# Feed-forward tail of a decoder layer: fetches, bias, last scale and expert number moved

## The chip, the cores and the metric

The kernel runs on one NeuronCore of a Trainium2 chip. The metric is device time in microseconds of one execution. The engines are PE (TensorE, matmuls), DVE (VectorE), ACT (ScalarE), POOL (GpSimd) and SP (SyncE, which here only issues DMAs). Each works through its own list of instructions in order; semaphores tie them together.

## The reference

A decoder layer: self-attention, cross-attention, and a feed-forward block with a choice of two of eight experts per token, each followed by a residual sum and a layer norm. There are 16 x 100 = 1600 tokens of width 512. What the change touches is the last part:

```
logits = x @ router_w + router_b                 # [tokens, 8]
topk_vals, topk_idx = top_k(logits, 2)
full_w = softmax weights of the two, 0 elsewhere
h = einsum('td,edf->etf', x, expert_w) + expert_b
combined = einsum('etf,te->tf', silu(h), full_w)
out = combined @ proj_w + proj_b
y = x + out
ffn = norm_w * (y / sqrt(mean(y * y) + 1e-6))
result = layernorm(x + ffn)
```

## The kernel before

`build` runs three phases one behind the other, with all engines meeting in between: `self_attention_phase`, `cross_attention_phase` and `feed_forward_phase`. Only the third concerns us in detail. Its input x2 lies in HBM. It has these stages.

**Routing.** PE transposes x2 and makes the logits; DVE ranks them, counts tokens per expert and gives each (token, choice) a slot. The slots fill NJ = 32 tiles of 128, and all slots of a tile belong to one expert, whose number is in `te_s`. In the meantime the weights are loaded and each is split in a high and a low fp32r half (`Ehl`, `Phl`); a product of two split matrices takes three matmuls (high x high, low x high, high x low).

**Expert stage**, a loop over the 32 tiles. POOL gathers the tile's rows of x2 by an indirect DMA (`gather_slots`, three buffers). PE transposes them (L1304, four at 128x128), ACT casts the result to the high half (`slots_hi`, L1364), DVE makes the low half (`slots_lo`, L1514). PE's iteration j is: transposes of tile j+1, a wait for the low half of tile j (`g_lo`), the load of the expert's number into a register (`value_load`, L1314), then four quarters (`c`) of three matmuls each (L1317 to L1319), whose weights are addressed by that register. DVE adds the expert's bias (L1526), ACT takes Silu (L1373), SP stores the tile to `y_d` in HBM (L1247). ACT's order is: high half of tile j+1, Silu of tile j.

**Output stage**, a loop over NT = 13 tiles of tokens (the last has 64). It begins when all 32 tiles have been stored. SP loads x2 once more (`x2r`, four DMAs, L1251), and with it the bias `pb_s` and the norm weight `nw_s`, each spread over 128 partitions (L1253, L1254). POOL gathers the two expert results of each token (`gather_results`, L1604, two indirect DMAs per tile). The steps on a tile t are, with their engine:

- ACT: `weigh_first` (L1378), weight of the first result; DVE: `combine` (L1532), adds the second one weighted
- PE: `transpose_combined` (L1326); ACT: `combined_hi` (L1384); DVE: `combined_lo` (L1538)
- PE: `product3` (L65), twelve matmuls with 512 columns
- POOL: `biased_residual` (L1610), x2 plus bias; DVE: `residual` (L1545), adds the product
- ACT: `square` (L1390), with a sum over the row; POOL: `rms` (L1615, L1617), adds eps and takes the power -0.5 of a single column
- DVE: `rms_norm` (L1551 to L1558), scale, x2 added, statistics; POOL: `ln` (L1622, L1624), the same for the variance
- DVE: `layer_norm` (L1563), subtracts the mean and scales; SP: store to the output (L1257)

The order on each engine is written out by hand, as a software pipeline. In step t DVE does combine(t+1), combined_lo(t), residual(t-1), rms_norm(t-2), layer_norm(t-3). POOL issues the gathers of tiles 0 to 2, then biased_residual(0) and (1), then in step t gather(t+3), biased_residual(t+2), rms(t-1), ln(t-2). The tiles of the output stage lie where the expert weights were, so they can be filled only after the last expert matmul.

## Time and profile before

| | us |
|---|---|
| median of 3 runs (lowest, highest) | 1701.53 (1699.75, 1701.56) |
| the profiled execution | 1697.03 |
| its span | 1695.2 |
| mean granted clock of PE | 0.94 of full |
| PE busy | 1492.5, 88% of the span |
| DVE busy | 1001.7, 59% |
| POOL busy | 688.0, 41% |
| ACT busy | 647.0, 38% |

The profile is of one execution. All times inside it count from the first instruction. Shares over the whole span say little about a change at the end of the program; the feed-forward phase begins near 1371 us, its expert stage runs from 1475 to 1591, and its output stage from there to the end. Matmuls overlap in the records: with 0.39 each they start 0.23 apart.

### The profile page before, as it was taken

Reading aid. Unit: us, or ns where it says so; the run is one execution under the profiler, and the core shown is the slowest. Engines: PE = TensorE matmul, PEld = TensorE weight load, DVE = VectorE, ACT = ScalarE, POOL = GpSimd, SP = SyncE. Lnnn points to the kernel's source line nnn. Section 1 sums busy time; section 2 is a strip of 40 time slices with the busy share of each in tenths; the row PEclk is TensorE's granted clock in tenths of the full one; section 3 lists DMA queues with packets and bytes.
Section 4 is the critical chain, followed back from the end, with each engine's and each line's share of the span. In section 5 each row is a group of like instructions: output and inputs, shape, how many; then the busy total and the mean of one; then the engine's idle time right before and its main releaser. Section 6 shows DMA issues by size and latency. Waiting matters only on the chain. (4 is left out here: it accounts for less than half of the span.)

```text
span 1695.2 us, 27877 instructions
## 1 busy us (share of the span) xinstructions
PE 1492.5 (88%) x8420; PEld 1227.9 (72%) x8420; DVE 1001.7 (59%) x3594; ACT 647.0 (38%) x1744; POOL 688.0 (41%) x1041
## 2 busy tenths in 40 slices
PE   7999999999975899999999999999999962599665
PEld 6778787787754678788887878878788862477443
DVE  3765666656654755566565666555566517633388
ACT  4433434434321544344444344444344413233222
POOL 1343332423323544444444434444444207422186
PEclk9999999999987999999999999999999965599788
DMA  6212112121115311111111111111111044255532
GB/s 215 98 51 97 68 68 87 58 96 58 73 69 173 115 52 62 57 53 47 57 56 59 59 53 49 55 57 61 57 57 47 31 139 181 74 149 149 196 112 84
DMA packets 59538, 143.21 MB, mean 84 GB/s; under 512 B 7038, under 2 KB 17890, under 8 KB 58459
## 3 DMA queue, kind: packets, MB, share of 16 engines
q1 hardware_dynamic: 54878, 127.36, 22.1%
q0 software_dynamic: 4576, 14.95, 3.5%
q8 instruction: 27, 0.44, 0.1%
q14 instruction: 57, 0.46, 0.1%
HBM read 97.85 MB, written 44.43 MB: 84 GB/s over the span
## 5 line engine op out<-in xcount | busy, mean ns | idle before, releaser
L65 PE MATMUL b_bank<-b_kTh,b_q 128*100 128x362 f32 x512 | 172.0, 337 | 6.6 <-DVE b_nmax L963 4.0
L876 ACT ACTIVATE b_probs<-b_probs,b_nmax 100x361 f32<-100x361 f32 x256 | 151.8, 593 | 65.6 <-DVE b_nmax L963 64.4
L1064 POOL TENSOR_TENSOR b_pcarry<-b_half 128x1 f32<-128x1 f32 x176 | 41.7, 237 | 314.5 <-DVE b_rinv L969 261.3
L963 DVE CUSTOM_DVE_ANT_0 b_probs<-b_bank,b_mask 100x361 f32<-100x361 f32 x256 | 135.5, 529 | 50.7 <-issue 39.6
L1089 POOL TENSOR_SCALAR b_probs<-b_probs,b_rinv 100x361 f32<-100x361 f32 x256 | 158.3, 631 | 0.0
L956 DVE TENSOR_TENSOR b_pTl<-b_bank,b_pTh 121x400 fp32r<-121x400 f32 x192 | 110.0, 573 | 50.2 <-ACT b_pTh L871 48.8
L871 ACT ACTIVATE b_pTh<-b_bank 121x400 fp32r<-121x400 f32 x192 | 96.7, 504 | 100.3 <-PE b_bank L740 99.2
L903 ACT ACTIVATE b_oTh<-b_bank,b_bv 128x400 fp32r<-128x400 f32 x64 | 38.1, 595 | 209.5 <-PE b_bank L65 209.5
L740 PE MATMUL b_bank<-b_ident,b_probs 100*121 100x100 f32 x768 | 110.7, 267 | 4.9 <-POOL b_probs L1089 4.9
L740 PEld LDWEIGHTS b_bank<-b_ident,b_probs 100*121 100x121 f32 x768 | 108.5, 187 | 7.3 <-POOL b_probs L1089 6.3
L65 PE MATMUL b_bank<-b_Woh,b_oTh 128*100 128x512 f32 x256 | 108.1, 422 | 1.4 <-DVE b_oTl L1028 1.4
L65 PEld LDWEIGHTS b_bank<-b_kTh,b_q 128*100 128x100 f32 x512 | 85.2, 166 | 28.0 <-issue 9.5
L1028 DVE SCALAR_TENSOR_TENSOR b_oTl<-b_bank,b_bv,b_oTh 128x400 fp32r<-128x400 f32 x64 | 40.5, 633 | 107.9 <-ACT b_oTh L903 107.9
L65 PE MATMUL a_bank<-a_Wqh,a_x1Th 128*100 128x512 f32 x256 | 101.5, 396 | 2.7 <-DVE a_qn L472 1.5
L65 PE MATMUL a_bank<-a_Wqh,a_x1Tl 128*100 128x512 f32 x256 | 101.6, 397 | 0.0
L65 PE MATMUL a_bank<-a_Wql,a_x1Th 128*100 128x512 f32 x256 | 101.3, 396 | 0.0
L65 PE MATMUL b_bank<-b_Wol,b_oTh 128*100 128x512 f32 x256 | 101.1, 395 | 0.0
L65 PE MATMUL b_bank<-b_Woh,b_oTl 128*100 128x512 f32 x256 | 101.0, 394 | 0.0
L65 PE MATMUL b_bank<-b_Wkh,b_ctxh 128*121 128x512 f32 x192 | 83.8, 437 | 14.6 <-DVE b_Wkl L918 14.6
L357 ACT ACTIVATE a_probs<-a_probs,a_nmax 100x100 f32<-100x100 f32 x256 | 92.8, 365 | 4.4 <-DVE a_nmax L425 4.4
L540 POOL TENSOR_TENSOR a_probs<-a_probs,a_rinv 100x400 f32<-100x400 f32 x64 | 54.7, 855 | 95.0 <-DVE a_rinv L432 95.0
L65 PE MATMUL b_bank<-b_kTl,b_q 128*100 128x362 f32 x256 | 84.4, 330 | 0.0
(238 smaller groups left out, 4066.0 us busy)
## 6 DMA issues: line engine op xcount, KB each, us to landing
q_d<-a_qo SPq DMA_DIRECT2D x64, 400.0 KB, 2.4
b_q<-q_d SPq DMA_DIRECT2D x64, 400.0 KB, 3.1
b_ctxr<-in_ctxT SPq DMA_DIRECT2D x48, 242.0 KB, 4.0
c_stage<-in_expert_w SPq DMA_DIRECT2D x16, 512.0 KB, 5.9
y_d<-c_y SPq DMA_DIRECT2D x32, 256.0 KB
a_stage<-in_Wq SPq DMA_DIRECT2D x4, 1024.0 KB, 5.6
b_stage<-in_Wo SPq DMA_DIRECT2D x8, 512.0 KB, 3.5
...
```

The costliest lines, as they stand in the source:

```text
L65: mm = eng.matmul(out, lhsT=l(c), rhs=r(c), start=first and k == 0, stop=last and k == n - 1)
L357: e = act.activation(probs[:, r, c, :], probs[:, r, c, :], ACT.Exp, scale=-1.0, bias=nmax[:, h:h + 1], accum_out=psums[:, r, c:c + 1])
L540: pool.tensor_tensor(probs[:, r], probs[:, r], rinv[:, r].unsqueeze(2).to_broadcast([S, DC, S]), ALU.mult).then_inc(pn_rdy, 1)
L740: mm = pe.transpose(t_bank[c % 2][0:KT, h * S:(h + 1) * S], probs[:, s % 2, h, c * KT:(c + 1) * KT], ident_s[0:S, 0:S])
L871: act.activation(pTh[:, c, :], t_bank[c % 2][0:KT, 0:XG * S], ACT.Copy).then_inc(pt_hi, 1)
L876: act.activation(p, p, ACT.Exp, scale=-1.0, bias=nmax[:, s % 2, h:h + 1], accum_out=psums[:, s % 2, h:h + 1]).then_inc(e_rdy, 1)
L903: act.activation(oTh[:, kv, :], o_bank[:, 0:XG * S], ACT.Identity, bias=bv_s[:, kv:kv + 1]).then_inc(o_hi, 1)
L956: dve.tensor_tensor(pTl[:, c, :], t_bank[c % 2][0:KT, 0:XG * S], pTh[:, c, :].bitcast(F32), ALU.subtract).then_inc(pt_lo, 1)
L963: dve.tensor_tensor_reduce(out=probs[:, s % 2, h, 0:SE], in0=s_bank[h % 2][0:S, 0:SE], in1=mask_s[:], scale=-1.0, scalar=BIG, op0=ALU.add, ...
L1028: dve.scalar_tensor_tensor(out=oTl[:, kv, :], in0=o_bank[:, 0:XG * S], scalar=bv_s[:, kv:kv + 1], in1=oTh[:, kv, :].bitcast(F32), op0=ALU.add,
L1064: pool.tensor_tensor(pcarry[:, k:k + 1], half_s[:, 0:1], half_s[:, 0:1], ALU.add)
L1089: pool.tensor_scalar(p, p, rinv[:, s % 2, h:h + 1], 1.0, ALU.mult, ALU.mult).then_inc(p_rdy, 1)
```

## The change

Five edits, all but one within `feed_forward_phase`:

- **x2.** The first three tiles (`x2a`) are loaded during the expert stage, behind the first store; the other ten (`x2b`) after it in three DMAs of three tiles and one of the rest. `residual` waits per group of three tiles.
- **Bias.** `pb_s` is one row. ACT casts it and a row of ones after the second Silu (behind a wait for both loads), DVE makes the low half, and each product gets two more matmuls with a contraction of one row (`ones_r` x `pbh`, `ones_r` x `pbl`). `biased_residual` is gone; `residual` adds x2 to the product.
- **Small steps.** The two additions of eps move from POOL to DVE (`mean_square` and the end of `rms_norm`); POOL keeps the two powers, with ln ahead of rms.
- **Last scale.** ACT does it, with a scale and a shift; DVE makes the shift, one column (`mean_shift`).
- **Expert number.** The load for tile j+1 stands ahead of the last quarter of tile j.

The semaphores of the first phase are cleared on POOL ahead of the second and given back ahead of the third. Several tiles now share memory with ones used up earlier.

```diff
+            def expert(j):
+                return pe.value_load(te_s[0:1, j:j + 1], min_val=0, max_val=E - 1)
+
             transpose_slots(0)
+            e_next = expert(0)
             pe.wait_ge(w_lo, NP)
             for j in range(NJ):
+                e = e_next
                 if j + 1 < NJ:
                     transpose_slots(j + 1)
                 pe.wait_ge(g_lo, j + 1)
                 wait(pe, h_rdy, j - 1)
-                e = pe.value_load(te_s[0:1, j:j + 1], min_val=0, max_val=E - 1)
                 for c in range(DC):
+                    if c == DC - 1 and j + 1 < NJ:
+                        e_next = expert(j + 1)
...
@@ SP @@
-                if j == NJ - 1:
-                    sp.wait_ge(h_done, NJ)
-                    for k in range(4):
-                        sp.dma_start(held(x2r, k), four_tiles(x2_f, k)).then_inc(x2r_in, 16)
-                        if k == 0:
-                            sp.dma_start(pb_s[:], proj_b.partition_broadcast(P)).then_inc(tail_in, 16)
-                            sp.dma_start(nw_s[:], norm_w.partition_broadcast(P)).then_inc(tail_in, 16)
+                if j == 0:
+                    sp.dma_start(pb_s[:], proj_b.rearrange("(a d) -> a d", a=1)).then_inc(tail_in, 16)
+                    sp.dma_start(nw_s[:], norm_w.partition_broadcast(P)).then_inc(tail_in, 16)
+                    sp.dma_start(x2a[:], x2_f[0:3 * P, :].rearrange("(t p) d -> p t d", p=P)).then_inc(x2_in[0], 16)
+            sp.wait_ge(h_done, NJ)
+            for k in range(3):
+                sp.dma_start(x2b[:, 3 * k:3 * k + 3], x2_f[(3 + 3 * k) * P:(6 + 3 * k) * P, :].rearrange("(t p) d -> p t d", p=P)).then_inc(x2_in[k + 1], 16)
+            sp.dma_start(x2b[0:rows(NT - 1), NT - 4], x2_f[(NT - 1) * P:B * S, :]).then_inc(x2_in[0], 16)
...
@@ PE, output stage @@
-                         lambda c: Phl[:, 0, c, :], lambda c: Phl[:, 1, c, :], range(DC)).then_inc(p_done, 1)
+                         lambda c: Phl[:, 0, c, :], lambda c: Phl[:, 1, c, :], range(DC), last=False)
+                pe.matmul(p_bank[t % 2][0:n, :], lhsT=ones_r[:, 0:n], rhs=pbh[:], start=False, stop=False)
+                pe.matmul(p_bank[t % 2][0:n, :], lhsT=ones_r[:, 0:n], rhs=pbl[:], start=False, stop=True).then_inc(p_done, 1)
...
@@ ACT @@
+                if j == 1:
+                    act.wait_ge(tail_in, 32)
+                    act.activation(ones_r[:], ones_s[0:1, :], ACT.Copy).then_inc(pb_split, 1)
+                    act.activation(pbh[:], pb_s[:], ACT.Copy).then_inc(pb_split, 1)
...
+            def layer_norm(t):
+                n = rows(t)
+                act.wait_ge(shift_set, t + 1)
+                act.activation(u_s[0:n, t], u_s[0:n, t], ACT.Identity, scale=rstd[t][0:n, :], bias=shift[t][0:n, :]).then_inc(o_rdy, 1)
...
@@ DVE @@
-                dve.wait_ge(x2p_set, t + 1)
-                dve.tensor_tensor(u_s[0:n, t], p_bank[t % 2][0:n, :], u_s[0:n, t], ALU.add).then_inc(u_rdy, 1)
+                if t == NT - 1:
+                    dve.wait_ge(x2_in[0], 48)
+                elif t % 3 == 0:
+                    dve.wait_ge(x2_in[t // 3], 32)
+                dve.tensor_tensor(u_s[0:n, t], p_bank[t % 2][0:n, :], x2_tile(t), ALU.add).then_inc(u_rdy, 1)
...
+            def mean_square(t):
+                n = rows(t)
+                dve.wait_ge(sq_done, t + 1)
+                dve.tensor_scalar(rr[t][0:n, :], ss[t][0:n, :], D * RMS_EPS, None, ALU.add).then_inc(ms_set, 1)
...
+                dve.wait_ge(mv_set, t + 1)
+                dve.tensor_scalar(rstd[t][0:n, :], mv[t][0:n, 1:2], LN_EPS, None, ALU.add).then_inc(var_set, 1)
...
+            def mean_shift(t):
+                n = rows(t)
+                dve.wait_ge(rstd_set, t + 1)
+                dve.scalar_tensor_tensor(out=shift[t][0:n, :], in0=mv[t][0:n, 0:1], scalar=-1.0, in1=rstd[t][0:n, :], op0=ALU.mult,
+                                         op1=ALU.mult).then_inc(shift_set, 1)
...
@@ POOL @@
-            pool.wait_ge(tail_in, 32)
-            biased_residual(0)
-            biased_residual(1)
             for t in range(NT + 2):
                 if t + 3 < NT:
                     gather_results(t + 3)
-                if t + 2 < NT:
-                    biased_residual(t + 2)
+                if 2 <= t:
+                    ln(t - 2)
                 if 1 <= t <= NT:
                     rms(t - 1)
-                if t >= 2:
-                    ln(t - 2)
...
@@ build @@
+        for handle in first:
+            nc.gpsimd.sem_clear(handle)
         cross_attention_phase(nc, sem, a["ctxT"], a["Wk"], a["Wv"], a["Wo"], a["bk"], a["bv"], a["mask"],
                               a["ident"], x1_d, q_d, x2_d)
+        for handle in first:
+            nc.release_semaphore(handle)
```

In the lists below a row is a line of the kernel, an operation, what it writes and reads (`c_te` holds the expert numbers, `c_xg` the gathered slots, `c_xgh` and `c_xgl` their two halves, `c_Ehl` the expert weights) and its size. The lines of the changed kernel have other numbers. On PE, at the border between two expert tiles, there stood before:

```order
L1317 MATMUL c_bank<-c_Ehl,c_xgh 128x512
L1318 MATMUL c_bank<-c_Ehl,c_xgl 128x512
L1319 ISA
L1319 MATMUL c_bank<-c_Ehl,c_xgh 128x512
L1304 MATMUL c_bank<-c_ident,c_xg 128x128 x4
L1314 TENSOR_LOAD c_te
L1314 ISA x2
L1317 ISA
L1317 MATMUL c_bank<-c_Ehl,c_xgh 128x512
```

and stands now:

```order
L1336 MATMUL c_bank<-c_Ehl,c_xgh 128x512
L1319 TENSOR_LOAD c_te
L1319 ISA x2
L1334 ISA
L1334 MATMUL c_bank<-c_Ehl,c_xgh 128x512
L1335 MATMUL c_bank<-c_Ehl,c_xgl 128x512
L1336 ISA
L1336 MATMUL c_bank<-c_Ehl,c_xgh 128x512
L1315 MATMUL c_bank<-c_ident,c_xg 128x128 x4
L1334 ISA
L1334 MATMUL c_bank<-c_Ehl,c_xgh 128x512
```

The load went from behind the transposes to ahead of the last three matmuls of the tile before.

On DVE one step of the output stage was (`c_r` results, `c_bank` the product, `c_u` the row under way, `c_small` single columns, `c_x2r` and `c_x2b` copies of x2):

```order
L1532 SCALAR_TENSOR_TENSOR c_r<-c_r,c_small 128x512
L1538 TENSOR_TENSOR c_cTl<-c_bank,c_cTh 128x512
L1545 TENSOR_TENSOR c_u<-c_bank,c_u 128x512
L1551 SCALAR_TENSOR_TENSOR c_u<-c_u,c_small,c_nw 128x512
L1554 TENSOR_TENSOR c_u<-c_u,c_x2r 128x512
L1556 BN_STATS c_stat<-c_u 128x6
L1558 BN_AGGR c_small<-c_stat 128x2
L1563 TENSOR_SCALAR c_u<-c_u,c_small 128x512
```

and is now:

```order
L1569 TENSOR_TENSOR c_cTl<-c_bank,c_cTh 128x512
L1584 TENSOR_SCALAR c_small<-c_small 128x1
L1579 TENSOR_TENSOR c_u<-c_bank,c_x2b 128x512
L1604 SCALAR_TENSOR_TENSOR c_small<-c_small 128x1
L1590 SCALAR_TENSOR_TENSOR c_u<-c_u,c_small,c_nw 128x512
L1593 TENSOR_TENSOR c_u<-c_u,c_x2b 128x512
L1595 BN_STATS c_stat<-c_u 128x6
L1597 BN_AGGR c_small<-c_stat 128x2
L1599 TENSOR_SCALAR c_small<-c_small 128x1
L1563 SCALAR_TENSOR_TENSOR c_r<-c_r,c_small 128x512
```

The last wide operation is gone (it is on ACT), and three operations of one column have come in.

On POOL the beginning of the output stage was:

```order
L1591 DMA c_xg<-x_d,c_tok 128x512 x32
L1604 DMA c_r<-y_d,c_slot 128x512 x6
L1610 TENSOR_TENSOR c_u<-c_x2r,c_pb 128x512 x2
L1604 DMA c_r<-y_d,c_slot 128x512 x2
L1610 TENSOR_TENSOR c_u<-c_x2r,c_pb 128x512
L1604 DMA c_r<-y_d,c_slot 128x512 x2
L1610 TENSOR_TENSOR c_u<-c_x2r,c_pb 128x512
L1615 TENSOR_TENSOR c_small<-c_small 128x1
L1617 TENSOR_TENSOR c_small<-c_small 128x1
```

and is now:

```order
L1636 DMA c_xg<-x_d,c_tok 128x512 x32
L1649 DMA c_r<-y_d,c_slot 128x512 x10
L1655 TENSOR_TENSOR c_small<-c_small 128x1
L1649 DMA c_r<-y_d,c_slot 128x512 x2
L1660 TENSOR_TENSOR c_small<-c_small 128x1
L1655 TENSOR_TENSOR c_small<-c_small 128x1
L1649 DMA c_r<-y_d,c_slot 128x512 x2
```

The ten gathers of tiles 0 to 4 now follow each other directly, and two operations of one column per tile remain.

## Rows read from the trace of the kernel before

**Rows 1.** Windows: length; PE, PEld, DVE, ACT, POOL busy (count); clock, DMA share, GB/s.

```profile
1482.00:1590.00 108.00, 101.36 (x485) 80.58 (x483) 41.52 (x60) 33.84 (x61) 25.12 (x27) 1.00 0.50 142
...
1621.00:1672.00 51.00, 36.34 (x137) 26.60 (x138) 50.18 (x67) 15.14 (x34) 45.66 (x59) 0.87 0.37 115
```

**Rows 2.** Timeline of PE, expert stage: start us, us, engine line, [idle before <-releaser].

```profile
1488.09 0.47 PE L1317 MATMUL c_bank<-c_Ehl,c_xgh 128*128 x1
...
1491.96 0.49 PE L1317 MATMUL c_bank<-c_Ehl,c_xgh 128*128 x1 [0.43 <-issue]
...
1495.18 0.47 PE L1317 MATMUL c_bank<-c_Ehl,c_xgh 128*128 x1
```

**Rows 3.** PE sequencer at the lines L1314 and L1317: durations ns, first and last start.

```profile
L1314 PEldq TENSOR_LOAD <-c_te x1: 859/859/859, 1490.7 to 1490.7; - x1
...
L1317 PEldq FUSED_REGOPS  x1: 46/46/46, 1488.8 to 1488.8; - x1
```

**Rows 4.** Timeline, same stretch: what feeds the PE's next tile.

```profile
1495.13 0.69 DVE L1526 TENSOR_TENSOR c_h<-c_bank,c_eb 128x512 f32<-128x512 f32 x1 [1.33 <-PE c_bank L1319]
...
1497.01 0.69 DVE L1514 TENSOR_TENSOR c_xgl<-c_bank,c_xgh 128x512 fp32r<-128x512 f32 x1 [1.18 <-ACT c_xgh L1364]
```

**Rows 5.** Timeline of PE: first matmul of expert tiles 1 and 31.

```profile
1481.03 0.48 PE L1317 MATMUL c_bank<-c_Ehl,c_xgh 128*128 x1
...
1586.90 0.49 PE L1317 MATMUL c_bank<-c_Ehl,c_xgh 128*128 x1
```

**Rows 6.** Timeline at expert tiles 0 and 1, then DMA issue by line, us to landing.

```profile
1482.35 3.52 SPq L1247 DMA_DIRECT2D y_d<-c_y  x2
...
1484.89 0.63 ACT L1373 ACTIVATE c_y<-c_h 128x512 f32<-128x512 f32 x1 [2.09 <-DVE c_h L1526]
...
c_nw<-in_norm_w SPq DMA_DIRECT2D x1, 256.0 KB, 6.8
```

**Rows 7.** Timeline at the start of the output stage.

```profile
1610.75 2.53 POOL L1610 TENSOR_TENSOR c_u<-c_x2r,c_pb 128x512 f32<-128x512 f32 x2 [9.15 <-DMA c_x2r<-x_d]
...
1612.13 0.69 DVE L1545 TENSOR_TENSOR c_u<-c_bank,c_u 128x512 f32<-128x512 f32 x1 [2.82 <-POOL c_u L1610]
...
1613.43 0.97 POOL L1604 DMA_INDIRECT c_r<-y_d,c_slot  x1
...
1618.12 0.72 ACT L1378 ACTIVATE c_r<-c_r,c_small 128x512 f32<-128x512 f32 x1 [4.53 <-DMA c_r<-y_d,c_slot]
...
1618.87 2.30 DVE L1532 SCALAR_TENSOR_TENSOR c_r<-c_r,c_small 128x512 f32<-128x512 f32 x1 [6.04 <-ACT c_r L1378]
```

**Rows 8.** Timeline of DVE and POOL, one tile of the output stage.

```profile
1629.91 2.14 DVE L1563 TENSOR_SCALAR c_u<-c_u,c_small 128x512 f32<-128x512 f32 x1
1630.48 1.27 POOL L1610 TENSOR_TENSOR c_u<-c_x2r,c_pb 128x512 f32<-128x512 f32 x1
...
1632.17 0.98 POOL L1617 TENSOR_TENSOR c_small<-c_small 128x1 f32<-128x1 f32 x1
...
1634.12 1.33 POOL L1604 DMA_INDIRECT c_r<-y_d,c_slot  x1 [0.18 <-issue]
...
1636.06 0.18 DVE L1558 BATCH_NORM_AGGREGATE c_small<-c_stat 128x2 f32<-128x6 f32 x1
...
1636.16 2.15 DVE L1563 TENSOR_SCALAR c_u<-c_u,c_small 128x512 f32<-128x512 f32 x1
```

**Rows 9.** Chain that ended last: start us, us, what; then POOL's drain at the end.

```profile
1675.12 0.65 DVE c_r L1532
...
1690.21 0.54 DVE c_u L1563
...
L1132 POOLq DRAIN  x1: 5406/5406/5406, 1689.6 to 1689.6; - x1
```

**Rows 10.** POOL and its queue where the second phase begins.

```profile
530.04 0.19 POOL L1064 TENSOR_TENSOR b_pcarry<-b_half 128x1 f32<-128x1 f32 x1 [12.65 <-DMA b_ctxr<-in_ctxT]
...
L76 POOLq EVENT_SEMAPHORE  x2: 17/17/17, 526.3 to 526.4; - x2
```

72 lines of the change are left out of this document (40 added, 32 removed).

## The prediction, made before the changed kernel was run

> **What bounds the kernel now.** I read the windows by stage first. The last phase starts near 1371 us, and the change touches only its last two stages: the expert stage (32 tiles of slots) and the output stage (13 tiles of tokens). In the expert stage PE is busy 101 of 108 us at the full granted clock; in the output stage DVE is busy 50.2 of 51 us while PE has 36 and POOL 46 [rows 1]. So PE sets the first and DVE the second.
>
> Next I read the PE timeline of two expert tiles. The tile that starts at 1488.09 lasts 3.87 us and the next 3.22, the long one with a gap of 0.43 before the following tile's first matmul that nothing in the profile releases ("issue") [rows 2]. PE's sequencer shows why. The load of the expert's number starts at 1490.7 and takes 0.86 us [rows 3]; with the two register operations behind it the first matmul comes 1.25 us after the load's start. The load stands behind the wait for the low half of the tile's own slots. In the tile that PE starts at 1495.18, DVE takes up the result of the one before at 1495.13 and, after ACT, has the next low half ready at 1497.01 + 0.69 = 1497.70 [rows 4], 2.52 us into a tile that needs 3.22. A load that starts only then shows its first matmul at 1498.95 at the earliest, 0.6 late. A tile delayed in this way gives the following load more time, which then hides. Hence a long and a short tile in turn. First matmuls run from 1481.03 to 1586.90, 30 tiles in 105.87 us, 3.53 each [rows 5].
>
> In the output stage I read the timeline at its start and in its middle. At the start POOL stands at the sum of x2 and bias until all of x2 has landed (9.15 us idle, ends 1610.75), and the gathers for tile 3 are queued behind it: they are issued at 1613.43, ACT gets the data at 1618.12, and DVE, idle for 6.04 us, goes on at 1618.87 [rows 7]. In the middle a DVE step repeats every 6.25 us (1629.91 to 1636.16). Of it 2.14 is the last scale L1563, beside POOL's L1610 of 1.27 [rows 8]; with POOL quiet the same line takes 0.54 [rows 9]. The rest of the step is 4.10.
>
> **The expert number, part by part.** The load now stands ahead of the last quarter of the tile before. At that point the sequencer is ahead of the array: the register operation of the last quarter is at 1488.8 in the short tile [rows 3], and its matmul comes nine matmuls after 1488.09, about 1490.24, so the lead is 1.4 us against a cost of 1.2 (the load and what follows up to the next dispatch). Then the wait for DVE no longer holds up a load, only matmuls, and it ends some 0.7 us before the PE has finished the tile before. Every tile should take the short 3.22: 30 x 3.22 = 96.6, a gain of 9.3, and 0.65 once more for the first tile, together 10.0. Nothing else becomes late: DVE's low half comes 2.52 us into a tile of 3.22 [rows 2, 4].
>
> **Loads and casts in the expert stage.** SP issues three more DMAs behind the first store (1482.35), and ACT, after the second Silu (1484.89, 0.63), waits for two of them and then casts a row of ones and the bias. Norm weights took 6.8 us to land, next to 3 MB of x2 [rows 6]. The issue now falls at about 1483, with little traffic, so I take 4 us (bounds 3 and 6.8). ACT then waits about 1.5 to 2 us, works 0.8, and queued behind it is the high half of tile 3, on which DVE's low half and PE hang. Of about 2.8 us the slack of 0.65 is hidden: cost 2.2 once (bounds 0.2 and 5). SP's stores behind it have two tiles of time. The early x2 load (768 KB) is hidden by PE-bound tiles. The 58 semaphore clears on POOL at the start of the second phase are new. POOL waits there from 526.4 to 530.04 for a DMA anyway; at 17 ns, the nearest row, they take 1.0 us, and at 62 ns they would fill the 3.6 [rows 10]. I take nothing, upper bound 2.
>
> **Start of the output stage.** POOL no longer stops at the bias, so it issues the gathers of tiles 0 to 4 one after another; those of tile 3 have landed by about 1608. The first residual waits for PE rather than POOL, and the two one-row matmuls per tile cost 2 x 0.23 at full clock (a twelfth of a short tile less its transposes; bound 0.43 each at half). I leave it at 1612.2 [rows 7]. Then ACT squares tile 0 (up to 0.8) after DVE's 0.69, weighs tile 3 (0.72), and DVE combines it at about 1614.5 in place of 1618.87: gain 4.3. PE needs 12 x 0.23 + 0.46 = 3.2 us for product 1 from about 1612.5, so it is ready as DVE comes to residual 1, and what is late next is the DVE step itself.
>
> **The DVE step.** It loses 2.15 (L1563 goes to ACT, which is busy 15 of 51 us [rows 1] and has room for 0.7 per 4.7). It gains three one-column operations. The aggregate L1558 starts 0.10 before its successor [rows 8], and a dependent one costs about twice that: 0.5 together (bounds 0.3 and 0.75). That makes 4.10 + 0.5 = 4.6. POOL's step is near that too: two gathers (1.33 and 0.97 with gaps of 0.3), a power beside a DVE operation 0.98, the other about 0.57 [rows 7, 8], 4.45. PE needs 0.35 + 14 x 0.23 = 3.6, at half clock about 7. I take 4.75. In the profile combines 3 and 12 stand at 1618.87 and 1675.12 [rows 7, 9], nine steps of 6.25; at 4.75 the gain is 13.5 (bounds 4.4 and 5.3: 16.6 and 8.5).
>
> **The end.** From combine 12 to the end of the span are 20.1 us, of which the last 5.4 are POOL's drain, after the last power [rows 9]. Four steps each lose 0.54 and gain 0.5, and with no combine left the powers on POOL are not covered: two or three waits of 0.6. Cost 1.5 (bounds 0 and 3).
>
> A rule bears on the step. The rows show one-column powers of POOL stretched (0.98) beside DVE, and DVE's wide operations not. The Trainium skill (SBUF — State Buffer, "SBUF: two separate sides") says that the port pair DVE and GpSimd share is held for a whole instruction, also between a DVE operation with two SBUF inputs and a GpSimd one that reads SBUF, and that the loser blocks whoever it is. By it DVE too would wait for powers that start first, and the sum would be the third rival's below.
>
> **Sum.** -10.0 + 2.2 - 4.3 - 13.5 + 1.5 = -24.1 us. Against the profiled execution of 1697.03 (span 1695.2 and 1.8 around it) that is 1672.9. The median of the runs shown is 4.5 higher, 1701.53, so the forecast is 1677.4.
>
> **The rivals.** First, the load stays exposed: if the matmuls are held not by the load but by the low half itself, long and short tiles remain and 10.0 comes back: 1687.4. For it speaks that the load starts right at DVE's end; against it that the short tile shows 1.25 us between the two. Chance 0.12.
>
> Second, POOL's ring limits the step. The mean square on DVE releases a power, behind it stand two gathers, then 4.7 us from the pair's start to the weighing [rows 7], then the combine, in two steps. That is 1.4 + 0.7 + 4.7 + 0.7, near 8 of 9.5, with 0.5 more by stretches. Should the data land 2.5 later, the step is 5.3: 9 x 0.55 = +5.0, 1682.4. Chance 0.12.
>
> Third, DVE blocks behind POOL's powers, about 0.57 in each of 12 steps: +6.8, 1684.2. Against it: DVE's wide operations beside L1617 are not longer in this profile. Chance 0.08.
>
> Fourth, the block on DVE just moves from L1563 to another line, so the step stays 6.25: +13.5, 1690.9. Against it: the blocker L1610 is gone altogether. Chance 0.04.
>
> Fifth, slower: the load stops PE inside each accumulation. If the sequencer has hardly any lead before the last quarter (0.1 us), 31 tiles lose 1.1 us each, +34: 1711.5. It decides from a lead under 0.4 us, where 31 x 0.8 eats the whole sum. The short tile's lead of 1.4 speaks against it [rows 3]. Chance 0.04. By the Trainium skill (TensorE: Matmul & The Clock Gate, the table at its head) PE's queue holds 64 instructions, which would leave room for such a lead; the row shows a lead of six matmuls and their weight loads.
>
> Last, 0.05 for better than 1670 (step 4.4, no stop of ACT, earlier landings), and 0.55 for the forecast.
>
> **How the numbers follow.** The range runs from 1670 to 1689: the forecast with its bounds and the first three rivals, 0.87 less some for bounds that add up. A measurement of this kernel can tell about 0.2% (3.4 us) from no change. Faster by more than that is every case but the fifth and a sliver: 0.94; within, 0.02; slower, 0.04.
>
> **What would show it.** Expert tiles all near 3.2 us with no "issue" gap, load starts well before DVE's low half; one gap of about 2 us at tile 3. In the output stage no DVE wait of 6 us before combine 3, a step of 4.75, no operation of DVE over 1 us, POOL nearly full. The prediction is wrong if a gap appears before the last quarter of each tile, if ACT waits for r data in each step, or if PE falls to its lower clock through the output stage.

## The result

The changed kernel takes 1681.15 us (median of 4 runs, 1676.13 to 1681.73) against 1700.64 for the kernel before, measured beside it (4 runs, 1698.10 to 1701.56): ratio 0.9881, interval 0.9859 to 0.9904, 19.5 us less. The same pair, measured once more with the experiments, gave 1677.78 (5 runs, 1671.51 to 1683.35) against 1702.01 (11 runs), ratio 0.9846 (0.9826 to 0.9866), 24.2 us less. The forecast was 1677.4, in a range from 1670 to 1689. The first result lies 3.8 above it and the second 0.4; both are in the range.

One execution of each measurement was profiled; the last column of the table is that of the second one. The first of the changed kernel took 1681.01 us (span 1679.2). Where a stage starts and ends was read from the timeline in the same way for both. The marks are the barriers between phases, the start of the first matmul of the expert stage and of the last one on its first line (L1317, now L1334), and the combines on DVE, which count the output tiles.

| stage, us | before | changed | changed, again |
|---|---|---|---|
| first two phases, to the barrier's end | 1371.0 | 1378.1 | 1380.5 |
| last phase to first expert matmul | 104.3 | 102.9 | 103.5 |
| expert stage | 113.8 | 107.3 | 107.0 |
| to combine 0 | 14.4 | 14.4 | 14.4 |
| combine 0 to combine 3 | 15.4 | 10.5 | 10.3 |
| combine 3 to combine 12 | 56.1 | 44.3 | 44.2 |
| combine 12 to the last barrier's end | 20.1 | 21.6 | 21.5 |
| last phase in all | 324.1 | 301.0 | 300.9 |

The last phase lost 23.1 us. Phases one and two, in which only the semaphore clears are new, seem to have taken 7.1 back; below it turns out that most of this is scatter, the profiled execution of before being the fastest one of its kernel.

Windows of the changed kernel by stage, the expert stage and then combine 3 to 12 (length; PE, PEld, DVE, ACT, POOL busy with counts; clock, DMA share, GB/s); they answer to [rows 1]:

```profile
1481.00:1588.30 107.30, 104.56 (x501) 86.20 (x502) 42.87 (x62) 36.88 (x65) 26.50 (x28) 0.96 0.54 155
1613.20:1657.50 44.30, 40.76 (x169) 27.96 (x168) 40.24 (x89) 22.83 (x45) 30.86 (x33) 0.96 0.47 133
```

PE still sets the expert stage (104.6 of 107.3 busy), at a granted clock of 0.96 of full. In the output stage DVE is busy 40.2 of 44.3 us, no longer all of it, and PE's share has gone up to 40.8. PE's idle times end with DVE's combine, so DVE still sets the step, but PE is close behind.

Timeline of PE in the expert stage, the first matmul of tiles 2 to 5 (answers to [rows 2]):

```profile
1489.72 0.48 PE L1334 MATMUL c_bank<-c_Ehl,c_xgh 128*128 x1
...
1495.88 0.49 PE L1334 MATMUL c_bank<-c_Ehl,c_xgh 128*128 x1 [2.73 <-DVE c_xgl L1545]
...
1500.67 0.48 PE L1334 MATMUL c_bank<-c_Ehl,c_xgh 128*128 x1
...
1503.84 0.48 PE L1334 MATMUL c_bank<-c_Ehl,c_xgh 128*128 x1
```

The last two are 3.17 apart, and the tiles from there on come every 3.17 to 3.22: the long ones and the "issue" gaps of [rows 2] are gone. One gap stands out, 2.73 us before the tile at 1495.88, and that tile lasts 4.79 although nothing waits in it: the clock record shows half clock (1.2 GHz) for 3.4 us, from 0.4 behind the gap's end. The load itself, as PE's sequencer had it before (L1314) and has it now (L1319), durations in ns as minimum, median and maximum:

```profile
L1314 PEldq TENSOR_LOAD <-c_te x32: 307/848/863, 1474.4 to 1586.1; - x32
```

```profile
L1319 PEldq TENSOR_LOAD <-c_te x32: 297/302/499, 1478.2 to 1583.5; - x32
```

Timeline of ACT and DVE around the gap (answers to [rows 4] and [rows 6]):

```profile
1490.40 0.63 ACT L1393 ACTIVATE c_y<-c_h 128x512 f32<-128x512 f32 x1 [2.06 <-DVE c_h L1557]
...
1493.71 0.31 ACT L1396 ACTIVATE c_ones_r<-c_ones 1x128 fp32r<-1x128 f32 x1 [2.67 <-DMA c_nw<-in_norm_w]
1493.92 0.61 ACT L1397 ACTIVATE c_pbh<-c_pb 1x512 fp32r<-1x512 f32 x1
1494.44 0.57 ACT L1384 ACTIVATE c_xgh<-c_bank 128x512 fp32r<-128x512 f32 x1
...
1495.05 0.69 DVE L1545 TENSOR_TENSOR c_xgl<-c_bank,c_xgh 128x512 fp32r<-128x512 f32 x1 [4.67 <-ACT c_xgh L1384]
```

ACT waits 2.67 us for the norm weight (issued at 1488.59, so landed 5.1 later), casts, and only then makes the high half, behind which DVE's low half and PE's next tile stand, in the order that the prediction gave.

Timeline at the start of the output stage (answers to [rows 7]):

```profile
1611.13 0.69 DVE L1579 TENSOR_TENSOR c_u<-c_bank,c_x2a 128x512 f32<-128x512 f32 x1 [3.71 <-PE c_bank L1358]
...
1612.49 0.71 ACT L1402 ACTIVATE c_r<-c_r,c_small 128x512 f32<-128x512 f32 x1
...
1613.23 0.75 DVE L1563 SCALAR_TENSOR_TENSOR c_r<-c_r,c_small 128x512 f32<-128x512 f32 x1 [1.41 <-ACT c_r L1402]
```

The wait of 6.04 us before combine 3 is gone, and ACT weighs tile 3 with no wait for data. Timeline of one undisturbed step in the middle, DVE with one POOL power (answers to [rows 8]):

```profile
1648.34 0.74 DVE L1563 SCALAR_TENSOR_TENSOR c_r<-c_r,c_small 128x512 f32<-128x512 f32 x1
...
1648.51 0.99 POOL L1660 TENSOR_TENSOR c_small<-c_small 128x1 f32<-128x1 f32 x1 [0.40 <-DVE c_small L1599]
...
1652.86 0.15 DVE L1599 TENSOR_SCALAR c_small<-c_small 128x1 f32<-128x1 f32 x1
1652.93 0.74 DVE L1563 SCALAR_TENSOR_TENSOR c_r<-c_r,c_small 128x512 f32<-128x512 f32 x1
```

The step is 4.59 us and no DVE operation exceeds 0.75. Not every step is so. At tile 8 the results that POOL gathers by the token's slots come late:

```profile
1637.82 0.72 ACT L1402 ACTIVATE c_r<-c_r,c_small 128x512 f32<-128x512 f32 x1 [2.13 <-DMA c_r<-y_d,c_slot]
...
1638.57 0.75 DVE L1563 SCALAR_TENSOR_TENSOR c_r<-c_r,c_small 128x512 f32<-128x512 f32 x1 [1.67 <-ACT c_r L1402]
```

Nine steps of 4.59 would be 41.3 us; they took 44.3. Of the 3.0 more, 1.8 fall on this step, 0.6 on a later one with a late gather, and 0.5 on the first, which takes 5.0 in every variant of the changed kernel. At the end of the kernel POOL's drain is the same 5.4 us as in [rows 9]:

```profile
L1132 POOLq DRAIN  x1: 5406/5406/5406, 1673.6 to 1673.6; - x1
```

### The profile page after: what moved, and what is told of

Its sections match the earlier page's. It is cut to its first block and busy times, and to the rows that moved or that the text cites. A ratio compares the mean times of both kernels' runs of the same rounds, so it can differ in the third digit from the quotient of the medians.

```text
span 1679.2 us, 27983 instructions
## 1 busy us (share of the span) xinstructions
PE 1495.3 (89%) x8446; PEld 1229.6 (73%) x8446; DVE 986.3 (59%) x3621; ACT 657.4 (39%) x1759; POOL 660.7 (39%) x1002
## 5 line engine op out<-in xcount | busy, mean ns | idle before, releaser
L1064 POOL TENSOR_TENSOR b_pcarry<-b_half 128x1 f32<-128x1 f32 x176 | 41.8, 238 | 319.6 <-DVE b_rinv L969 263.1
L740 PE MATMUL b_bank<-b_ident,b_probs 100*121 100x100 f32 x768 | 110.7, 267 | 5.0 <-POOL b_probs L1089 4.9
L65 PE MATMUL a_bank<-a_Wqh,a_x1Tl 128*100 128x512 f32 x256 | 101.7, 397 | 0.0
```

Of the source, the lines that this page charges most:

```text
L65: mm = eng.matmul(out, lhsT=l(c), rhs=r(c), start=first and k == 0, stop=last and k == n - 1)
L740: mm = pe.transpose(t_bank[c % 2][0:KT, h * S:(h + 1) * S], probs[:, s % 2, h, c * KT:(c + 1) * KT], ident_s[0:S, 0:S])
L1064: pool.tensor_tensor(pcarry[:, k:k + 1], half_s[:, 0:1], half_s[:, 0:1], ALU.add)
```

## The experiments

They went in three groups. In each, the kernel before was run beside them on the same chip (medians 1702.01, 1700.81 and 1701.69 us over 11, 17 and 11 runs). The changed kernel itself ran beside the first group alone (load back, casts late, scale on DVE). What is said below of the others' distance to it goes from group to group, whose medians of before differ by up to 1.2 us. All of the diffs are against the changed kernel but for the two that say otherwise, and show the main lines only; "..." marks what is left out. What is tested are the terms of the sum. The last table gives the stages of all of them.

### The changed kernel again

> The changed kernel again, as the yardstick for the runs beside it. Theory: about 1680 us, with the same stages as in its profile: the start of the cross-attention phase at 526 to 530 us by the luck of one store, expert tiles 3.18 us apart, an output step of 4.6 where no gather is late. Rival: the 3.9 us by which the first phase ended later in the profile of the changed kernel belong to the change; then they are here again.

Measured: 1677.78 us, 24.2 less than before. Its profiled execution was the slowest of its five (1683.35), and yet its last phase took 300.9 us, as the first one's 301.0: what differs between these two executions lies in the first two phases.

### The load behind the wait again

```
-            e_next = expert(0)
 ...
                 wait(pe, h_rdy, j - 1)
+                e = expert(j)
                 for c in range(DC):
-                    if c == DC - 1 and j + 1 < NJ:
-                        e_next = expert(j + 1)
```

> The changed kernel with the load of the expert's number back behind the wait for the low half. Theory (the load's 1.25 us after the wait is what made long tiles): long and short tiles return, 3.5 us a tile, and the time is 9 to 10 us above the changed kernel. Rival (the low half itself holds the matmuls, and tiles became even because other work moved): tiles stay at 3.2 and the time within 2 us.

Measured: 1690.78 us (6 runs), 13.0 more than the changed kernel; the expert stage 118.4 us, 11.4 more. PE's waits in the expert stage (waited for: us in total, times, longest):

```profile
PE c_bank L1331 <- DVE c_xgl L1542: 4.2, 2, 3.0
PE c_bank L1331 <- issue: 1.5, 6, 0.6
```

The rival fell: the early load is what made the tiles short. But they did not come back long and short in turn. From the fifth tile on they stand 3.20 to 3.72 us apart, 3.51 in the mean and most of them nearly even, so that few of the gaps are long enough for this list. What is the same is the sum of two tiles, near 7.05, against 7.07 in the kernel before. Part of the 11.4 is the clock: with the gap of 3.03 us the record shows half clock for 6.8 us, of which 1.1 lie in the gap itself. The other 5.7 cost 2.9, where the 3.4 of the changed kernel cost 1.7. That leaves 10.2 for the load.

### The load early, in the kernel before

Against the kernel before, with nothing else of the change: the load in the same place as in the changed kernel.

```
 ...
+            e_next = expert(0)
             pe.wait_ge(w_lo, NP)
             for j in range(NJ):
+                e = e_next
 ...
-                e = pe.value_load(te_s[0:1, j:j + 1], min_val=0, max_val=E - 1)
                 for c in range(DC):
+                    if c == DC - 1 and j + 1 < NJ:
+                        e_next = expert(j + 1)
```

> The kernel before with one part of the change alone: the expert's number is loaded ahead of the last quarter of the tile before. Theory (the term on record): all tiles take 3.2 us, the expert stage shrinks by 10.0, so 10 us faster than before, ratio 0.9941; no wait of ScalarE for a load exists in this kernel, so nothing of it is given back there. Rival A (half of each pair of tiles is held by something else, as the low half): 5 us or less. Rival B (the later stages take some back, as the output stage starts while x2 is still landing, on which POOL's sum waits there): the expert stage gives 10, the kernel only 5 to 8.

Measured: 1689.67 us (6 runs), ratio 0.9936 (0.9922 to 0.9949), 12.0 less than before's 1701.69. This measures the term by itself, and both rivals fall: the expert stage shrank from 113.8 to 102.2 us, by 11.6, and the later stages (15.3, 55.9 and 20.1) gave nothing back. Of the 11.6, some is chance: the stage begins at half clock in every profile, here for 3.2 us and before for 5.4, and each of these microseconds costs half of one. Without it the load is worth 10.5. Windows of the first 8 us and the rest of this kernel's stage, and its load:

```profile
1477.50:1485.50 8.00, 7.96 (x33) 6.48 (x33) 2.18 (x4) 3.00 (x4) 1.88 (x2) 0.80 0.35 84
1485.50:1579.70 94.20, 94.20 (x471) 77.95 (x470) 40.70 (x59) 33.10 (x59) 24.57 (x26) 1.00 0.57 158
```

```profile
L1308 PEldq TENSOR_LOAD <-c_te x32: 296/301/490, 1474.8 to 1575.0; - x32
```

PE has no idle time from tile to tile. The load moved out of the wait also became cheaper, 0.30 us in the median where it had 0.85. With the load back behind the wait, in the experiment above, it had 0.85 again.

### The casts later

```
-                if j == 1:
+                if j == 8:
                     act.wait_ge(tail_in, 32)
```

> The changed kernel with ACT's wait for the bias and norm weight and the two casts after tile 8 in place of tile 1. Theory: the loads have landed by then, ACT works 0.8 us more instead of stopping for 2.7, PE's gap of 2.7 us at tile 2 and its 3.4 us at the lower clock behind it (1.8 us lost) go; a gap of 0.2 at tile 9 stays: 4 us below the changed kernel. Rival: the gap is the slot gather, not ACT; then nothing changes.

Measured: 1677.39 us (4 runs), 0.4 less than the changed kernel: no difference, where 4 was expected. The timeline of ACT names what took the wait's place:

```profile
1498.67 0.63 ACT L1393 ACTIVATE c_y<-c_h 128x512 f32<-128x512 f32 x1 [4.16 <-DMA y_d<-c_y]
```

ACT has two buffers for y. Tile 1's, whose store SP issued at 1490.88, lands 7.71 us later, since the loads of norm weight and x2 stand ahead of it on SP's queue, and tile 3's Silu needs its buffer. PE's gap is 1.33 us there, and its clock did not fall. The expert stage did shrink to 104.4 us in the profile: by the last table 1.1 for the shorter gap and most of the rest for the clock. Combine 0 to 3 took 1.1 to 1.3 more in the same profile, so the last phase came out at 300.7, where the changed kernel has 301.0 and 300.9. The load-back kernel has as much more there, and why stays open. The cast's wait was the first of two with the same cause.

### The loads spread, the casts later

```
-                if j == 0:
+                if j == 1:
                     sp.dma_start(pb_s[:], ...).then_inc(tail_in, 16)
+                if j == 4:
                     sp.dma_start(nw_s[:], ...).then_inc(tail_in, 16)
-                    sp.dma_start(x2a[:], x2_f[0:3 * P, :]...).then_inc(x2_in[0], 16)
+                if j in (7, 10, 13):
+                    k = (j - 7) // 3
+                    sp.dma_start(x2a[:, k], x2_f[k * P:(k + 1) * P, :]).then_inc(x2_in[0], 16)
 ...
-                if j == 1:
+                if j == 12:
                     act.wait_ge(tail_in, 32)
 ...
```

> The changed kernel with the tail's loads spread over the expert stage: bias row at tile 1, norm weight at tile 4, the three x2 tiles one each at tiles 7, 10 and 13, and ScalarE's two casts of the bias at tile 12. The two runs before it said that ScalarE's wait for the weight (2.7 us) costs a gap of PE of 2.7 and half clock behind it, and that with the casts alone moved, the y store queued behind the loads holds Silu by 4.2 us instead. Theory (both waits are landings behind that burst of loads): no gap of PE over 0.5 us in the expert stage, its first matmul to its last 102.5 instead of 107.0, 4.5 us faster than the changed kernel. Rival A (any load of 256 KB beside the stores of y holds one of them): three small gaps of 1 to 2 us, 1 to 3 us faster. Rival B (scatter of the stores hides it): within 1 us.

Measured: 1674.56 us (5 runs), 3.2 less than the changed kernel; the ratios to before, 0.9845 (0.9827 to 0.9864) and 0.9846, were measured in different groups and don't part them. The profile does: the expert stage takes 101.7 us, 5.3 less. All that ACT waits for in it (us in total, times, longest; the 21.4 lies ahead of the stage):

```profile
ACT c_y L1396 <- DVE c_h L1560: 66.6, 32, 3.0
ACT c_xgh L1387 <- PE c_bank L1318: 22.4, 2, 21.4
```

No DMA is among them, and PE has neither a gap nor half clock once its clock has risen. So the burst of loads behind the first store is the cause of both waits. Of the 5.3 us, 2.6 are the gap, 1.7 the half clock behind it, and the last 1.0 is the clock's rise at the stage's start, which came earlier here (half clock for 2.2 us, not 4.3) and is no effect of the edit that I can name.

### The last scale on DVE again

```
 ...
-                dve.scalar_tensor_tensor(out=shift[t][0:n, :], in0=mv[t][0:n, 0:1], scalar=-1.0, ...)
+                dve.tensor_scalar(u_s[0:n, t], u_s[0:n, t], mv[t][0:n, 0:1], rstd[t][0:n, :], ALU.subtract,
+                                  ALU.mult).then_inc(o_rdy, 1)
 ...
```

> The changed kernel with the last scale back on DVE at the end of its step, where the kernel before has it, and no shift column. Theory (the 2.15 us of that line were 0.5 of work and 1.6 of waiting behind POOL's sum of x2 and bias, which is gone): the line takes 0.54, the step grows from 4.6 to 5.0, and the time is 4 to 5 us above the changed kernel. Rival (the line is slow by itself beside any POOL work, as its gathers): it takes 1.5 to 2.1 again and the time is 15 to 18 us above.

Measured: 1682.19 us (5 runs), 4.4 more than the changed kernel, as expected. DVE in one step:

```profile
1634.53 0.59 DVE L1602 TENSOR_SCALAR c_u<-c_u,c_small 128x512 f32<-128x512 f32 x1
1635.05 0.73 DVE L1561 SCALAR_TENSOR_TENSOR c_r<-c_r,c_small 128x512 f32<-128x512 f32 x1
```

The step is 5.11 us (1629.42 to 1634.53). The operation that lasted 2.14 us in the kernel before takes 0.59 here, in the same place of the step. Of the 1.66 us by which the step shrank, from 6.25 to 4.59, moving the scale to ACT gave only 0.5, and 1.1 came with POOL's sum of x2 and bias gone: 1.55 of standing still, less what the small operations new on DVE cost. The rival, that any work of POOL makes this line slow, fell; POOL issues a gather beside it here too.

### POOL's sum put back, unused

```
 ...
+            pool.wait_ge(x2_in[0], 32)
             for t in range(NT + 2):
                 if t + 3 < NT:
                     gather_results(t + 3)
+                if t < 9:
+                    n = rows(t + 2)
+                    pool.tensor_tensor(spare[0:n, t], x2a[0:n, 0], x2a[0:n, 1], ALU.add)
                 if 2 <= t:
                     ln(t - 2)
```

> The changed kernel with an added sum on POOL in each of nine steps of the output stage: two 128x512 tiles of x2, which nothing reads, at the place where POOL's biased residual stood before; the result is not used. It gives POOL the width of work that the change took away, without its place in the dependences. Theory (before the change VectorE was the only engine filled in a step, so POOL's sum cost nothing of its own except where both run two-input operations at once): 0 to 2 us slower than the changed kernel in all, no step over 4.9. Rival (POOL's wide sum and VectorE's operations slow each other, as its 1.86 against 1.23 at the start of cross attention hints): VectorE operations of 2 us and steps of 5.3 or more, 6 us or more slower. Should POOL's powers come late behind the sum (1.27 us), the steps grow by up to that, which the waits on POOL would name: 5.9, 11 us slower.

Measured: 1688.59 us (4 runs), 10.8 more than the changed kernel. The theory (0 to 2) fell, and the rival came true: the two slow each other, 6 us or more. One step in the timeline:

```profile
1632.03 2.22 DVE L1564 SCALAR_TENSOR_TENSOR c_r<-c_r,c_small 128x512 f32<-128x512 f32 x1
...
1632.41 1.27 POOL L1675 TENSOR_TENSOR c_spare<-c_x2a 128x512 f32<-128x512 f32 x1
...
1634.16 0.68 DVE L1570 TENSOR_TENSOR c_cTl<-c_bank,c_cTh 128x512 fp32r<-128x512 f32 x1
```

The combine now has 2.22 us in place of 0.74, and the step is 6.07 instead of 4.59: 1.48 more, all of it this one operation. (The profiled execution, 1684.38, is the fastest of the four; in it combines 3 to 12 take 7.2 more, and what the slower ones add is not shown.) Nothing waits for the sum's result; the sum alone does it. The combine ends 0.57 us behind the sum's end, nearly its whole own length, so it did next to nothing while the sum ran. With the scale on ACT the same 2.2 us fell on the next DVE operation that met the sum.

By the Trainium skill (SBUF — State Buffer, "SBUF: two separate sides") the port pair that DVE and GpSimd share is an exclusive lock, for a DVE operation with two SBUF inputs too where the GpSimd one reads SBUF, and the loser blocks. The trace agrees that DVE blocks. It doesn't show the page's order, by which the one that starts first wins: the combine's record starts 0.38 us ahead of the sum's and loses. The records may not show the true starts. In the kernel before, L1563 starts 0.57 us ahead of the sum that holds it [rows 8], and needs only 0.54 with POOL quiet, so by the records it would have been all but done. Against POOL's short powers it goes the other way: the combine that starts 0.17 to 0.38 us ahead keeps its 0.74, and the power ends some 0.43 behind it. What decides who is held stays open.

### The same sum between POOL's two powers

```
 ...
                 if 2 <= t:
                     ln(t - 2)
+                if t < 9:
+                    n = rows(t + 2)
+                    pool.tensor_tensor(spare[0:n, t], x2a[0:n, 0], x2a[0:n, 1], ALU.add)
                 if 1 <= t <= NT:
                     rms(t - 1)
 ...
```

> The changed kernel with the same nine unused sums of 128x512 on POOL as in the run before it, but each put between the two powers of a POOL step instead of ahead of both, so that it should run beside VectorE's operations that read PSUM (low half, residual) and not beside the combine or the others whose inputs all lie in SBUF. In the run before it, the combine that started 0.4 us before POOL's sum took 2.22 us instead of 0.74, and the step 6.07 instead of 4.59. Theory (it is the pair of all-SBUF operations on both engines that blocks VectorE): no VectorE operation over 1 us beside the sum; what is paid is only that the mean-square power comes 1.3 us later, some 0.3 to 0.7 of a step, steps of 5.0 to 5.4. Rival (any wide VectorE operation beside POOL's sum blocks): low half or residual of 2 us and steps of 6 as before.

Measured: 1682.75 us (4 runs), 5.8 less than with the sum ahead of the powers. One step:

```profile
1642.66 0.68 DVE L1570 TENSOR_TENSOR c_cTl<-c_bank,c_cTh 128x512 fp32r<-128x512 f32 x1
...
1643.15 1.28 POOL L1677 TENSOR_TENSOR c_spare<-c_x2a 128x512 f32<-128x512 f32 x1
...
1643.27 0.14 DVE L1585 TENSOR_SCALAR c_small<-c_small 128x1 f32<-128x1 f32 x1
1643.33 0.68 DVE L1580 TENSOR_TENSOR c_u<-c_bank,c_x2b 128x512 f32<-128x512 f32 x1
...
1643.92 0.53 DVE L1605 SCALAR_TENSOR_TENSOR c_small<-c_small 128x1 f32<-128x1 f32 x1
...
1644.98 0.75 DVE L1591 SCALAR_TENSOR_TENSOR c_u<-c_u,c_small,c_nw 128x512 f32<-128x512 f32 x1 [0.53 <-POOL c_small L1656]
```

The residual, which reads one input from PSUM, runs wholly beside the sum in its usual 0.68 us. The one-column operation behind it, with two inputs from SBUF, takes 0.53 in place of 0.15 and ends at 1644.45, just as the sum does (1644.43). The one ahead of the residual (L1585) has one input from SBUF, and runs beside the sum in its usual 0.14. The step is 5.49 us: 0.90 more than 4.59, made up of this 0.38 and a wait of 0.53 for the power that stands behind the sum, just over what was expected. The theory holds in the main: the same POOL operation blocks DVE's operations with two SBUF inputs, a narrow one too, and not one with an input in PSUM. Its words "all-SBUF" are too wide, as L1585 shows. They aren't too wide for every operation with one input: the scale L1563 of the kernel before has a single wide input besides its two columns, and was held.

### One clear for 58, and the clears alone

```
-        for handle in first:
-            nc.gpsimd.sem_clear(handle)
+        nums = sorted(handle.num for handle in first)
 ...
+        nc.gpsimd.sem_clear(range(nums[0], nums[-1] + 1))
```

> The changed kernel, but the 58 semaphore clears on POOL between the first two phases are one clear of a range. In its trace the 58 take 4.1 us (530.4 to 534.5) and PE's first matmul of cross attention stands 10.5 us behind the barrier instead of 8.6. Theory (the clears lie on the path, since all that follows in cross attention waits for POOL's first writes and gathers there): 1.9 us faster than the changed kernel. Rival A (other work hides them; the 1.9 is scatter of the DMAs): no difference, within 0.5 us. Rival B (all of the 7.1 us by which phase 2 ended later in the one profile comes from the clears): 5 us or more faster. The profile should show the first matmul of cross attention 8.6 us behind the barrier by the theory, 10.5 by rival A.

Measured: 1679.39 us (4 runs), 1.6 more than the changed kernel in the other group; ratios 0.9867 (0.9847 to 0.9886) and 0.9846 (0.9826 to 0.9866). No gain can be told. The queue did what it should (one execution each of the changed kernel and of this one):

```profile
L1697 POOLq EVENT_SEMAPHORE_RANGE_CLEAR  x58: 44/44/48, 530.4 to 534.5; - x58
```

```profile
L1698 POOLq EVENT_SEMAPHORE_RANGE_CLEAR  x1: 355/355/355, 529.3 to 529.3; - x1
```

POOL's first work in cross attention starts 2.7 us behind the barrier (532.01) in place of 4.3 or 4.4, while PE's first matmul stands at 9.5 (538.83) in place of 10.0 and 10.5. That distance doesn't follow the clears, though. It is 10.3 in the kernel before with the load alone, which has none of them, and 8.6 below with all 58. So the clears' 4.1 us lie in part under other waits, and the 10.5 are no sign of them. Then the kernel before with the clears alone:

```
 ...
+        for handle in first:
+            nc.gpsimd.sem_clear(handle)
         cross_attention_phase(
 ...
```

> The kernel before with one part of the change alone: semaphores of the first phase allocated on their own and cleared one by one on POOL before the second phase (58 clears). Theory: 1.9 us slower than before (POOL's clears hold the start of cross attention), all of it in the 10 us behind the first barrier. Rival A (my value on record): no difference. Rival B: 7 us slower, which is what the end of phase 2 shows between the two single profiles.

Measured: 1702.65 us (12 runs), ratio 1.0007 (0.9996 to 1.0017): 1.2 us more, between 0.7 less and 2.9 more. My zero and the theory's 1.9 both fit; the 7 us of rival B don't. The first matmul stands 8.6 us behind the barrier, as before. In the nine profiles of kernels with 58 clears whose other edits all lie in the last phase, the first two phases end at 1376.0 to 1380.5 us, with one clear at 1377.8 and 1375.1, with the clears alone at 1375.4, without any at 1371.0 and 1374.6. So most of the 7.1 us is the early end of this one profile of before; over whole runs the clears have 1.2 us, and zero is not excluded.

### The gathers one tile further ahead

```
 ...
-                wait(pool, r_w1, t - 3)
+                wait(pool, r_w1, t - 4)
 ...
-            for t in range(3):
+            for t in range(4):
                 gather_results(t)
 ...
-                if t + 3 < NT:
-                    gather_results(t + 3)
+                if t + 4 < NT:
+                    gather_results(t + 4)
 ...
```

> The changed kernel with POOL's gathers of results issued one tile further ahead of use (four tiles before the loop and t + 4 in it, five semaphores in place of four). In the profiles of the changed kernel the gather for tile 8 lands late in most (ScalarE waits 2.1 us for it) and one or two others by 0.4 to 0.9, so that combines 3 to 12 take 44.3 us instead of the 41.3 that nine steps of 4.59 give. Theory (the landing is the cause): these nine steps take 41.5 to 42.3, 2 to 2.8 us faster than the changed kernel. Rival A (POOL itself is late, since a step of POOL's own queue is nearly as long as DVE's, so that issuing further ahead finds the same place): no difference in the steps. Rival B: the fourth pair ahead comes at the start before combine 3 and holds the powers there: up to 2 us slower at the start, gain eaten.

Measured: 1675.39 us (4 runs), ratio 0.985 (0.9832 to 0.9869), 2.4 less than the changed kernel. Combines 3 to 12 take 41.8 us, 2.5 less than 44.3. All of ACT's waits from 1605 to 1665 us (combine 3 stands at 1608.7, combine 12 at 1650.5):

```profile
ACT c_junk L1414 <- DVE c_u L1579: 30.6, 13, 5.0
ACT c_u L1419 <- DVE c_small L1604: 2.3, 1, 2.3
```

No wait for a gather is left. Combine 0 to 3 takes 11.0, 0.5 to 0.7 more than in the changed kernel's profiles, but 10.3 to 11.7 occur without this edit, so no price at the start is shown. The theory is borne out by the profile with one reserve: the load-back kernel, whose output stage is the changed kernel's, had no gather later than 0.5 us either and took 42.1. Five profiles of this order of gathers have tile 8 late by 1.7 to 2.1, and the two with the edit none. The gain over whole runs is of the size of the scatter.

### All three

The spread loads, the gathers ahead and the one clear together.

> The changed kernel with three edits together: loads spread over the expert stage and casts late (measured alone, 3.2 us under the changed kernel's median), gathers one tile further ahead, one range clear for the 58 clears (measured alone, no difference that can be told). Theory: the two gains add up, since they lie in different stages: 2 us under the spread kernel's 1674.6, about 1672.6, ratio to before 0.983. Rival (the late gathers have another cause): the same as the spread kernel, 1674.6.

Measured: 1675.13 us (5 runs, 1672.44 to 1675.93), ratio 0.9844 (0.9832 to 0.9857). Not the 1672.6 expected, but what each of the first two gives alone. Combines 3 to 12 take 41.8 us as they should, 2.4 less than with the spread loads alone, yet the last phase is 295.4 us in both, since the expert stage takes 103.1 in place of 101.7 and the stretch to combine 3 takes 0.8 more. Windows of the first 8 us of the expert stage, in this kernel and then in the one with the spread loads:

```profile
1478.70:1486.70 8.00, 8.00 (x27) 6.32 (x27) 1.95 (x3) 2.89 (x4) 1.89 (x2) 0.68 0.30 72
```

```profile
1480.30:1488.30 8.00, 7.98 (x35) 6.54 (x35) 2.62 (x4) 3.00 (x4) 1.89 (x2) 0.86 0.39 104
```

The granted clock is 0.68 here and 0.86 there: half clock for 5.1 and 2.2 us. The difference of 2.9 us at half speed is 1.45, the whole of the stage's excess. So the two gains do add up in their own stages, and what hid the second in this profile is when the clock rises at the start of the expert stage, which differs from profile to profile also between kernels that are the same up to there. Whether it hid it in the other four executions isn't shown. Against the changed kernel's two medians this version is 2.7 and 6.0 us faster. It, the spread loads alone and the gathers alone are the best here, and the runs don't part the three.

### The stages of all kernels

From one profiled execution each, us; "median" is over all runs.

| kernel | median | expert stage | half clock in it, start + later | stage without it | combine 0 to 3 | combine 3 to 12 | last phase |
|---|---|---|---|---|---|---|---|
| before | 1700.64 to 1702.01 | 113.8 | 5.4 + 0 | 111.1 | 15.4 | 56.1 | 324.1 |
| clears alone | 1702.65 | 112.8 | 4.2 + 0 | 110.7 | 14.7 | 56.0 | 323.5 |
| load alone | 1689.67 | 102.2 | 3.2 + 0 | 100.6 | 15.3 | 55.9 | 310.6 |
| changed | 1681.15 | 107.3 | 5.1 + 3.4 | 103.1 | 10.5 | 44.3 | 301.0 |
| changed, again | 1677.78 | 107.0 | 4.3 + 3.4 | 103.2 | 10.3 | 44.2 | 300.9 |
| load back | 1690.78 | 118.4 | 4.5 + 6.8 | 112.8 | 11.7 | 42.1 | 312.4 |
| casts late | 1677.39 | 104.4 | 4.8 + 0 | 102.0 | 11.6 | 44.3 | 300.7 |
| scale on DVE | 1682.19 | 104.4 | 2.6 + 0 | 103.1 | 11.0 | 45.8 | 301.6 |
| one clear | 1679.39 | 107.3 | 5.0 + 3.4 | 103.1 | 10.4 | 44.1 | 302.9 |
| sum ahead of powers | 1688.59 | 104.6 | 2.2 + 0 | 103.5 | 10.6 | 51.5 | 306.2 |
| sum between powers | 1682.75 | 104.7 | 2.9 + 0 | 103.3 | 13.1 | 48.1 | 305.6 |
| spread loads | 1674.56 | 101.7 | 2.2 + 0 | 100.6 | 10.4 | 44.2 | 295.4 |
| gathers ahead | 1675.39 | 104.1 | 2.4 + 0 | 102.9 | 11.0 | 41.8 | 296.1 |
| all three | 1675.13 | 103.1 | 5.1 + 0 | 100.6 | 10.9 | 41.8 | 295.4 |

Half clock at the start is worked out from the window of the stage's first 8 us (length times one less the clock, times two), the later one is read from the clock record; "without it" takes off half of both. For load back it has 113.3 if the 1.1 us of half clock inside the gap are left out, as they should be. That column makes one picture of all kernels: 100.6 where nothing holds PE, that and the gap (1.3 to 2.9 us) where ACT is held, and some 10 more where the load stands behind the wait. It also shows when the gap is followed by half clock. Gaps of 2.7 to 3.0 us had it behind them in the four profiles where the clock had risen late (half clock for 4.3 us or more at the start). Gaps of 2.3 to 2.9 us did not in the four where it had risen early (2.9 or less), nor did casts late, where the clock rose late and the gap was 1.3. Why the start should matter stays open.

## Why the prediction was right

The time was right, and the mechanism in its large parts too, but some terms missed, in opposite directions. Term by term, as predicted and as the runs showed:

| term, us | predicted | shown | from |
|---|---|---|---|
| load early | -10.0 | -10.5 | the load alone, stage without half clock: 111.1 to 100.6 (whole kernel -12.0) |
| ACT held at the casts | +2.2 | +2.5 | the same column: 100.6 to 103.1 |
| half clock behind that gap | none | +1.7 | 3.4 us of it, in four of eight profiles with such a gap |
| start, to combine 3 | -4.3 | -4.9 | 15.4 to 10.5 |
| nine DVE steps | -13.5 | -11.8 | 56.1 to 44.3; undisturbed 4.59 each, -14.8 |
| end | +1.5 | +1.5 | 20.1 to 21.6 |
| clears | 0 | +1.2 | the clears alone (-0.7 to +2.9) |
| sum | -24.1 | -20.3 | measured -19.5 and -24.2 |

The terms as shown would give 1681.2 from the same base of 1701.53. That is the first measurement (1681.15), and the forecast's nearness to the second (0.4 us) is chance: its misses of 0.3 to 1.7 us had other signs in part, and the two medians of one kernel lie 3.4 apart. In the pair of profiles the last phase lost 23.1, of which the first six terms make 21.5. Of the rest 1.4 lie ahead of the first expert matmul, in a stretch that the change leaves alone and that varies by that much between profiles.

**The expert number.** The mechanism held in what the term rests on: the load was exposed behind the wait for the low half, and the short tile is what remains (3.18 to 3.19). The term was right to 0.5. Long and short tiles in turn are one form of it only. With the load back they came nearly even at 3.51, and in the kernel with the clears alone they went from 3.7 and 3.4 to 3.6 and 3.5. What the profiles have in common is the sum of two, near 7.07, 0.7 more than two short tiles. The lead of 1.4 us on which the fifth rival hung was enough.

**The hold of ACT.** The place and the order (norm weight, casts, high half, low half, PE) were right, and the gap of 2.73 is what I said within 0.5, though the norm weight took 5.1 us to land and not 4. I left out two things. One is that PE, once it stops, may go on at half clock: the tile behind the gap took 4.79 us instead of 3.18. I had noted half clock as a danger for the output stage only. The other didn't show until the casts were moved: the same loads, ahead of SP's stores of y, hold Silu. "SP's stores behind it have two tiles of time" was the wrong step, since one of these stores landed after 7.71 us, more than two tiles of 3.18.

**The start of the output stage.** Combine 3 was expected 4.3 earlier and came 4.9 earlier, for the reason given.

**The DVE step.** I took 4.75, worked out from 4.10 + 0.5 = 4.6 with something added for POOL. Undisturbed it is 4.59 and DVE is full. The mean over nine is 4.92. That it is 0.33 more comes from late gathers for the larger part (2.5 of 3.0 us in all, by the run that issues them earlier) and from the first step. Late data is the second rival's mechanism, at a third of its price: 0.17 a step above my 4.75 instead of 0.55. PE's need was mis-sized as well: 3.6, where it idles only 0.3 us a step in the run with the gathers ahead, so 4.3. It didn't matter, as DVE's 4.59 still hides it. I had put the whole 2.15 of L1563 down to that line. The experiments divide it otherwise: the scale costs 0.5, and the rest was DVE standing still while POOL's sum ran. Had the change moved the scale alone and kept the sum, the long operation would have been there with another name, which is the fourth rival; it failed here for the reason given against it, that the sum went too.

**The third rival**, DVE blocked behind POOL's powers, has nothing for it in the undisturbed step: it is POOL's power L1660 that takes 0.99 beside the combine (0.58 at tile 8, where no DVE operation runs beside it), and the combine keeps its 0.74.

**The clears.** I took nothing and gave 2 as the bound. They take 71 ns each from start to start, not the 17 of [rows 10], 4.1 us in all. Of this POOL's wait hid most: with the clears alone its first work comes 0.6 us later than before.

**The base.** The profiled execution of before was 4.5 us under its median, and the sum was carried over to the median. As far as the profiles go that was right: in the two other profiles of kernels with the old output stage, clears alone and load alone, the first two phases end 3.6 to 4.4 us later, while the stages behind the expert stage agree with before's within 1. The change hardly touches these phases.
